# Start-up loads, an early weight cast, the last transposes and the row gathers of a gated cross-attention and mixture-of-experts kernel

## The reference

```
h  = layernorm(x)                        # 32 x 128 x 512
q  = ((h @ Wq.T) per head @ w_kc_q) @ W_qr      # 16 heads, 64 wide
k  = rope(ctx) @ W_kr                            # 16 heads, 64 wide
o  = softmax(q k^T) @ rope(ctx) @ w_kv.T @ Wo.T
x1 = x + tanh(g0) * o
n  = layernorm(x1)
y  = sum over the two best of 8 experts (silu(gate) * up @ down, capacity 1280)
     + shared MLP (silu(gate) * up @ down, 1408 hidden)
out = x1 + tanh(g1) * y
```

## Time and profile before

| | |
|---|---|
| median of three runs | 1899.29 us |
| profiled execution: time / span | 1893.28 / 1891.5 us |
| PE busy | 1841.2 us (97% of the span) |
| DVE busy | 1163.3 us (62%) |
| ACT busy | 698.4 us (37%) |
| POOL busy | 688.3 us (36%) |
| chain that ended last | PE 83%, DVE 7%, ACT 3% |

### The profile page before, as it was taken

How to read it: one execution, slowest core, us unless ns; L and a number is a source line. 1 busy time by engine, 2 the same in 40 slices (tenths; PEclk the granted TensorE clock), 3 DMA queues, 4 the chain that set the end, 5 groups by cost and what they waited for, 6 DMA issues and landing times.

```text
span 1891.5 us, 34955 instructions
## 1 busy us (share of the span) xinstructions
PE 1841.2 (97%) x12946; PEld 1124.2 (59%) x12946; DVE 1163.3 (62%) x2294; ACT 698.4 (37%) x1978; POOL 688.3 (36%) x714
## 2 busy tenths in 40 slices
PE   7899999999999998999999999999999999999998
PEld 7556666666666564444455555555544567767676
DVE  5777777777777776475422222222236788888887
ACT  4566666666666666220122222222211111111111
POOL 3244555554555656100233334343355520110101
PEclk9999999999999999999999999999999999999999
DMA  8646666666666767513299998999943422221202
GB/s 278 161 104 132 132 138 147 145 137 145 128 144 133 166 148 163 144 44 111 77 198 238 251 218 213 219 215 220 208 136 130 123 79 67 68 90 34 78 23 90
DMA packets 478930, 268.47 MB, mean 142 GB/s; under 512 B 410704, under 2 KB 416464, under 8 KB 478800
## 3 DMA queue, kind: packets, MB, share of 16 engines
q1 hardware_dynamic: 467280, 228.90, 51.6%
q0 software_dynamic: 11520, 37.76, 7.1%
HBM read 118.72 MB, written 48.23 MB: 88 GB/s over the span
## 4 chain that ended last, share of the span: by engine, by line
PE 83%; DVE 7%; ACT 3%; issue 2%; POOL 2%; DMA 1%; SPq 1%; another core or an unknown queue 1%; DVEq 0%; ACTq 0%; POOLq 0%
PE o L635 14%; PE o L909 8%; PE p_bank L684 8%; PE score L898 8%; PE o L830 5%; PE score L781 5%; PE score L764 4%; PE p_bank L898 4%; PE m_bank L898 4%; PE m_bank L781 3%; PE p_bank L781 3%; PE t_bank L830 3%; PE c_bank L830 3%; DVE arena L1128 2%; PE p_bank L764 2%
## 5 line engine op out<-in xcount | busy, mean ns | idle before, releaser
L635 PE MATMUL o<-arena 128*128 128x512 bf16 x1536 | 352.4, 379 | 0.8 <-DVE arena L1128 0.8
L1128 DVE TENSOR_TENSOR arena<-arena 128x512 bf16<-128x512 f32 (+3 forms) x357 | 305.0, 861 | 14.6 <-ACT arena L1021 4.8
L1573 POOL TENSOR_TENSOR arena<-arena 128x512 f32<-128x512 f32 x128 | 150.6, 1176 | 301.3 <-DVE arena L1149 299.2
L986 ACT ACTIVATE arena<-score,arena 128x128 f32<-128x128 f32 x512 | 181.4, 370 | 160.1 <-DVE arena L1220 160.1
L635 PEld LDWEIGHTS o<-arena 128*128 128x128 bf16 x1536 | 147.7, 98 | 156.1 <-DVE arena L1128 1.6
L684 PE MATMUL p_bank<-arena 128*128 128x256 bf16 x1536 | 178.8, 273 | 0.8 <-DVE arena L1128 0.7
L1658 POOL TENSOR_TENSOR arena<-arena 128x1088 bf16<-128x1088 f32 x32 | 71.9, 2248 | 275.2 <-ACT arena L1011 275.2
L909 PE MATMUL o<-arena 128*128 128x512 bf16 (+1 forms) x720 | 168.4, 379 | 0.0
L684 PEld LDWEIGHTS p_bank<-arena 128*128 128x128 bf16 x1536 | 145.2, 98 | 24.5 <-DVE arena L1128 1.3
L898 PE MATMUL score<-arena 128*128 128x352 bf16 x960 | 151.5, 315 | 2.9 <-issue 2.9
L781 PE MATMUL score<-arena 128*128 128x256 bf16 x1152 | 144.0, 273 | 6.4 <-DVE arena L1503 4.5
(11 more groups left out here) (208 smaller groups left out, 3173.2 us busy)
## 6 DMA issues: line engine op xcount, KB each, us to landing
xrow_d<-arena SPq DMA_DIRECT2D x80, 256.0 KB
arena<-w_expert SPq DMA_DIRECT2D x32, 544.0 KB, 5.7
arena<-w_shared SPq DMA_DIRECT2D x22, 384.0 KB, 3.6
arena<-x SPq DMA_DIRECT2D x16, 512.0 KB, 4.9
arena<-x SPq DMA_DIRECT2D x32, 256.0 KB, 3.2
x_d<-arena SPq DMA_DIRECT2D x32, 256.0 KB, 2.6
xn_d<-arena SPq DMA_DIRECT2D x32, 256.0 KB, 2.5
arena<-x_d SPq DMA_DIRECT2D x8, 1024.0 KB
```

The costliest lines, as they stand in the source:

```text
L635: mm = pe.matmul(o_bank[b % 2][:, :], lhsT=cT[u % 2][:, a, h, :], rhs=M_w[:, w, head_of(hg, h), :], start=(hg == 0 and n == 0), stop=(hg = ...
L986: mm = act.activation(prob[:, u % 4, h, :], score_bank[u % 2][:, h * S:(h + 1) * S], ACT.Exp, bias=neg_max[:, u % 4, h:h + 1], accum_out=d ...
L1128: return dve.tensor_tensor(dst, src, hi, ALU.subtract)
L1573: pool.tensor_tensor(prob[:, u % 4], prob[:, u % 4], rden[:, u % 4, :].unsqueeze(2).broadcast_to([P, 4, S]), ALU.mult).then_inc(normed, 1)
```

## The change

There are four edits.

1. The first quarter of the A weights is loaded as one head and then three heads. The two loads of the first head have their own semaphore `wa_first`, which TensorE awaits for head 0; for head 1 it awaits `wa_in[0]`. x of the first blocks is issued behind `load_a(1)`. The first context and the rope tables are issued behind `load_a(2)`, `load_a(3)` and the first quarter of Wq.
2. ScalarE casts Wq of heads 8 to 15 and results 0 and 1 of B before the steps up to -13, so before it casts the normalized x. VectorE's and GpSimd's lists are as they were.
3. Blocks 29 and 31 have their `xT2` in `k_region`, blocks 28 and 30 in the old region. The transpose of 29 waits for `ct_mm` at its end and for `lg_mm` 28 (29 before); that of 30 for 29 (30 before); that of 31 for 30 (nothing before, but it stood behind the same `ct_mm` wait).
4. From g = 3 on, the gathers of a group are written as pairs in the steps m = 5, 6, 7, 8 in place of eight in step 5.

```
 def xT2(b):
-    region = xT2_region if b < NB - 1 else k_region[:, 5120:5888]
+    region = xT2_region if b < NB - 4 or b % 2 == 0 else k_region[:, 5120:5888]
...
 def turn_xn2(b, it):
     if within(b, NB):
-        wait(sp, lg_mm, b if b < NB - 1 else 0, 4, it)
+        wait(sp, lg_mm, b if b <= NB - 4 else b - 1, 4, it)
+        if b == NB - 3:
+            sp.wait_ge(ct_mm, NU)
...
-load_a(0)
+load_a(0, 0, 1)
+load_a(0, 1, 3)
+load_a(1)
 sp.dma_start(x_ln, x_g[0]).then_inc(xln_in, 16)
-load_a(1)
+load_a(2)
+load_a(3)
+load_wq(0)
 step(-23, None)
 sp.dma_start(table_sb, tables).then_inc(table_in, 16)
-load_a(2)
-load_a(3)
-for c in range(4):
-    heads = slice(4 * c, 4 * c + 4)
-    sp.dma_start(Wq_sb[:, heads, :], Wq_h[:, heads, :]).then_inc(wq_in[c], 16)
+for c in range(1, 4):
+    load_wq(c)
...
 # TensorE, A
-if h % 4 == 0:
+if half == 0 and h == 0:
+    pe.wait_ge(wa_first, 32)
+elif h % 4 == 0 or (half == 0 and h == 1):
     pe.wait_ge(wa_in[2 * half + h // 4], 32)
...
 # ScalarE
 upper_a(1)
+for h in range(8, 12):
+    upper_wq(h)
+for n in range(2):
+    upper_b(n)
+    upper_wq(12 + 2 * n)
+    upper_wq(13 + 2 * n)
 for k in range(FIRST_STEP, -12):
     step(k, None)
-for n in range(4):
-    upper_wq(8 + 2 * n)
-    upper_wq(9 + 2 * n)
+for n in range(2, 4):
     upper_b(n)
...
 # GpSimd
-def gather_rows(s, it):
+def gather_rows(s, it, rows=range(8)):
+    if 0 not in rows:
+        for i in rows:
+            gather_row(i)
+        return
...
-if v >= 34 and m == 5 and g < 8:
-    gather_rows(g, it)
+if v >= 34 and 5 <= m < 9 and g < 8:
+    gather_rows(g, it, range(2 * m - 10, 2 * m - 8))
```

More of the change, by code:

```diff
@@ L257, in build @@
         const_in, table_in = sem("const_in"), sem("table_in")
+        wa_first = sem("wa_first")
         wa_in = [sem(f"wa_in{i}") for i in range(4)]
@@ L476, in _, with load_a, load_wq @@
             W_qr4 = W_qr.rearrange("(t p) (c n) -> c p t n", t=3, c=4)
-            def load_a(c):
-                heads = slice(4 * c, 4 * c + 4)
-                sp.dma_start(wqk_sb[:, :, heads, :].rearrange("p t h k -> p t (h k)"), w_qk4[c]).then_inc(wa_in[c], 16)
-                sp.dma_start(wqr_sb[:, :, heads, :].rearrange("p t h r -> p t (h r)"), W_qr4[c]).then_inc(wa_in[c], 16)
-            load_a(0)
+            def load_a(c, first=0, n=4):
+                heads = slice(4 * c + first, 4 * c + first + n)
+                sp.dma_start(wqk_sb[:, :, heads, :].rearrange("p t h k -> p t (h k)"),
+                             w_qk4[c][:, :, first * P:(first + n) * P]).then_inc(wa_first if n == 1 else wa_in[c], 16)
+                sp.dma_start(wqr_sb[:, :, heads, :].rearrange("p t h r -> p t (h r)"),
+                             W_qr4[c][:, :, first * R:(first + n) * R]).then_inc(wa_first if n == 1 else wa_in[c], 16)
+            def load_wq(c):
+                heads = slice(4 * c, 4 * c + 4)
+                sp.dma_start(Wq_sb[:, heads, :], Wq_h[:, heads, :]).then_inc(wq_in[c], 16)
+            Wq_h = Wq.rearrange("(h k) d -> k h d", h=H)
+            load_a(0, 0, 1)
+            load_a(0, 1, 3)
+            load_a(1)
             sp.dma_start(x_ln, x_g[0]).then_inc(xln_in, 16)
-            load_a(1)
+            load_a(2)
+            load_a(3)
+            load_wq(0)
             step(-23, None)
             sp.dma_start(table_sb, tables).then_inc(table_in, 16)
-            load_a(2)
-            load_a(3)
-            Wq_h = Wq.rearrange("(h k) d -> k h d", h=H)
-            for c in range(4):
-                heads = slice(4 * c, 4 * c + 4)
-                sp.dma_start(Wq_sb[:, heads, :], Wq_h[:, heads, :]).then_inc(wq_in[c], 16)
+            for c in range(1, 4):
+                load_wq(c)
             sp.dma_start(kr_stage, W_kr).then_inc(kr_in, 16)
@@ L1721, in gather_rows, with gather_row @@
                 wait_first(now_done, s + 1, 2, it, 2 * TPX + 4 + s % 2)
[L1722 to L1725, removed]
+                for i in rows:
+                    gather_row(i)
+            def gather_row(i):
+                pool.indirect_dma_start(out=r_sb[:, i, :], out_offset=None, in_=xrow_d,
+                                        in_offset=bass.IndirectOffsetOnAxis(ap=slot_now[:, i:i + 1], axis=0))\
+                    .then_inc(r_in, 16)
             def shared_step(v, it):
```

## The result

The changed kernel takes 1907.53 us (median of six runs, 1907.15 to 1908.85) against 1898.62 before (1895.23 to 1901.72, six runs). The ratio is 1.0045 with a 95% interval of 1.0035 to 1.0056, so the change costs 8.5 us, within 6.6 to 10.6. The prediction said 1907.0, with a chance of 0.58 for slower.

A forecast was written before the change was run, and what follows sets the result against it. TensorE, busy 97% of the span, was taken as the bound, so early losses stay. Start +8.5 us (7.9 + 0.6), attention's end -0.8, gathers 0: +7.7, median 1899.3 to 1907.0 us; range 1900.5 to 1911.5.

The forecast's parts named there:

- signs named beforehand: A ends 26 to 26.5, rope near 21.9, B 31 to 32, VectorE idle 8 us, result 4 at 43 to 46.
- the three terms behind it: After B's start: x's first cast 5.5 us later, nine VectorE instructions 7.7 us, slower clock in results 4 to 7 +0.6.
- The load of three heads: Start-up: head 0 in at 4.2 us, heads 1 to 3 at 6.5 to 6.9, A ending about 1 us sooner.
- The rope ahead of Wq: GpSimd at start-up: late tables put the rope before four lowers, so B starts at 31.4, not 29.05; cost 2.35 us.
- ScalarE and VectorE: During B: VectorE waits for x's later cast, then nine instructions; result 4 at 44.6 instead of 36.68, +7.9 us.
- The clock: Results 4 to 7 of B run at TensorE's slower pace throughout after some 8 us idling: +0.6 us, bounds 0 and +2.
- The attention's end: Block 29's transpose goes earlier, then VectorE is late; the 3.86 us TensorE gap shrinks: -0.8 us.
- The alternative that I weighed: At the attention's end, shorter idling keeps TensorE's clock up; the sum would be about 1.8 us lower, left uncounted.
- The gathers: Expert groups: pairs still issue back to back, groups 4 to 7 unchanged, group 3's last lower moves; taken as 0.
- the bound of 2.4 us: Group 3's gather run: if its end causes VectorE's remote wait, the wait moves, between -2.4 and +2.4 us.

The follow-up runs named there:

- the split alone: Kernel before with only the first A load split into one and three heads, all other loads in the old order; ratio 1.0005, +0.9 us.
- the spaced version: Kernel before with gathers in pairs, those in steps m = 6, 7, 8 first waiting for VectorE's product of the step before; ratio 0.9965, -6.6 us.
- x early: Kernel before with the transposes edit, x cast and lowered before A's first half, Wq 8 to 15 before B's results, x's transposes before small loads; ratio 0.9978.
- VectorE lowering all: The x early kernel with VectorE writing the lower parts of all 16 heads of Wq and GpSimd none; ratio 0.9978, -4.2 us against the kernel before.
- VectorE in ScalarE's order: Changed kernel with VectorE's lowers of Wq 8 to 14 and results 0 and 1 ahead of x's; ratio 1.0027, +5.1 us against the kernel before.
- both together: Kernel before with x early, all Wq lowers on VectorE and spaced gathers; ratio 0.9945, -10.4 us, 1886.98 against 1897.58 us.
- the run with tables ahead: VectorE in ScalarE's order, plus first context and rope tables issued ahead of the last A quarter and Wq; ratio 1.0015, +2.9 us against the kernel before.

## Why the prediction was right

The direction, the size and the mechanism were right: the late rope and the unmoved list of VectorE, +7.7 said and +8.5 measured. How close the number came is in part luck. At the first projection the sum said +8.5 and the trace +8.75, but B started 1.6 us later than worked out, and the three terms behind it came out 1.4 us shorter together. Of the signs named beforehand, three were missed by the same error of the loads (the end of A, the landing of the tables, the start of B), and those on VectorE's wait, on result 4 and on the attention's end came true.

**The load of three heads (wrong).** The step said that heads 1 to 3 come when the quarter came, 6.5 to 6.9. They came at 8.4, A ended at 27.88 instead of 26.0 to 26.4, and all loads behind were 1.5 us later than worked out: Wq at 21.92 (20.4), tables at 23.39 (21.9). The run with the split alone shows that this is the split's doing (head 1 at 8.25, Wq at 23.12 against 21.78). The step allowed the split 0 to 0.4 us, and head 1 came 1.5 us behind the late end of that. Why the load of three heads is slow was not tried.

**The rope ahead of Wq (right, but placed too early by the loads' error).** It ran from 23.39 to 27.95, 4.6 us where I took 4.2. The four lowers took 4.82 us (5.2). B started at 32.98 instead of 31.4: the loads' 1.5 us and no more.

**ScalarE and VectorE (right).** x's first cast was ready 5.17 us after B's start (5.5); the nine instructions took 7.10 us (7.7). So result 4 was at 45.29 (44.6). The first three subtractions, beside GpSimd, took 3.48 and the six others 3.6: contention fell on three, not four, though GpSimd's rope went on to 44.57. The trace shows why it did not fall on more. Two of the later subtractions of arena operands started 0.14 us ahead of an operation of GpSimd, and then GpSimd's was the slow one, 1.12 and 1.07 us in place of 0.73:

```profile
42.16 0.67 DVE L1144 TENSOR_TENSOR arena<-arena 128x512 bf16<-128x512 f32 x1
...
42.30 1.12 POOL L1620 TENSOR_TENSOR arena<-arena 128x256 f32<-128x256 f32 x1
```

That VectorE's list is the cause is shown, not only argued: edit 2 alone costs 3.9 us at the first projection, and with VectorE's list in ScalarE's order result 4 starts 5.4 us sooner.

**The clock (right in direction, and not a fixed price).** I counted +0.6 for results 4 to 7 at the lower clock throughout. The clock was granted at 0.50 from 39.31 to 49.55, and they took 4.9 us (4.5 before); up to the first projection it is 4.72 against 4.58, +0.1. Results 0 to 3 took 4.26 (5.1 before), because the granted clock was up already from 35.90, but that gains nothing: result 4 waits for VectorE. The term stood on one profile, and the same instructions took 2.80 us in another execution with the old start-up.

**The attention's end (right).** -0.8 said; 0.7 in the gaps. That only VectorE's layernorm chain was then late is what the trace shows. The clock, left out of the sum, fell again for the same 3.41 us, so nothing was missed there. The alternative that I weighed, that the shorter idling keeps the clock up, held in one of seven profiled kernels with edit 3.

**The gathers (right).** The edit alone measured 0.9999, on a chip whose profiles lack the waits, and where they are there TensorE idles as long with it as without it. That the bound of 2.4 us stood for something real is shown by the spaced version. I had not asked what it would be worth to make the edit do what it says: 6.6 us.

## What to carry to other kernels

When one engine's list is reordered, read the lists of its partners: the casts were moved, VectorE's subtractions were not, and an engine that takes its work in order then stood 8.8 us behind one instruction. A load moved back in a queue delays whatever stands behind it in its consumer's list too, here the weights behind the rope. An edit that spreads instructions over steps of a written-out list does nothing unless each step has a wait of its own. And a start-up time read from one profile is to be checked against a second profile of the same instructions: here the clock alone moved it by 1.6 us.

## What the runs showed of the hardware

- Splitting a 1152 KB load into 288 and 864 KB made the whole arrive 1.0 to 1.9 us later (7.81 to 8.42 us in five profiles, against 6.47 to 6.84 in the eight that load it whole), though its first part came some 2.7 us sooner (3.71 to 3.82).
- Subtractions of two arena operands (128x512) take 0.61 us each in a row on VectorE alone (4.90 for eight) and 1.43 with GpSimd doing the same beside them, whose own take 1.51 (1.16 at their best in the earlier trace rows). Shared out between the two engines they go no faster than on VectorE alone (5.86 us for eight heads). Where the two engines' operations overlap singly, the one that started second was the slow one (0.67 us beside 1.12, above).
- The granted clock behind the same idling (2.46 or 2.47, then 0.94 to 1.08 us, at the attention's end) was 0.50 for 3.41 us in three of the seven profiled kernels with edit 3 (the changed one, x early, VectorE lowering all), for 6.83 us in three (edit 3 alone, VectorE in ScalarE's order, both together), and 1.00 throughout in the run with tables ahead, where eleven matmuls took 2.54 us instead of 4.90 in edit 3 alone. One kernel's profile cannot price this. Six of the twelve executions other than that of the kernel before had a fall that began between 69 and 79 us, after which TensorE was 1.5 us later, and the one of the kernel before had none.
- Runs of eight gathers from GpSimd came with waits of VectorE of 1.7 to 3.6 us that the profile calls remote in all seven profiles of unspaced kernels from the two slower groups and from the first result; in the four of the first group there was none, with the same runs of gathers, and the kernel before was 12.6 us faster there than in the second group. Spacing the gathers removed all of them but one. So the runs of gathers are needed for the waits and do not suffice. What the wait itself is, and what differs between the chips, was not tried.
